# Attention over gathered edges: values weighed from the gathered rows in SBUF, PSUM banks cleared by ScalarE

## The reference, cut to what matters

```python
q = (h @ Wq).reshape(n, H, DK)
k = (h @ Wk).reshape(n, H, DK)
v = (h @ Wv).reshape(n, H, DV)
e = jnp.sum(q[dst] * k[src], axis=-1) / np.sqrt(DK)
m = jax.ops.segment_max(e, dst, num_segments=n)
a = jnp.exp(e - m[dst])
z = jax.ops.segment_sum(a, dst, num_segments=n)
msg = v[src] * (a / (z[dst] + 1e-09))[:, :, None]
agg = jax.ops.segment_sum(msg, dst, num_segments=n)
```

## Time and profile before

| | before |
|---|---|
| median of 3 runs | 6919.58 us (6911.33 to 6929.57) |
| the profiled execution, its own time | 6900.21 us |
| its span | 6898.5 us |
| granted TensorE clock, mean | 0.895 of full |
| TensorE busy (matmul) | 5202.9 us, 75% |
| VectorE busy | 2801.3 us, 41% |
| GpSimd busy | 2226.9 us, 32% |
| ScalarE busy | 1456.7 us, 21% |
| first attention | 2972.3 to 3827 us |
| second attention | 3981 to 4851 us |

### The profile page before, as it was taken

The page is one execution under the profiler, slowest core; times in us unless marked ns, Lnnn a source line. Parts: engine busy times, 40 slices in busy tenths (PEclk is TensorE's granted clock), DMA queues, the critical chain, the costliest instruction groups (busy, mean ns, idle before and its releaser), DMA issues. The chain is left out here.

```text
span 6898.5 us, 86638 instructions
## 1 busy us (share of the span) xinstructions
PE 5202.9 (75%) x22758; PEld 3404.8 (49%) x22807; DVE 2801.3 (41%) x6714; ACT 1456.7 (21%) x3735; POOL 2226.9 (32%) x2209
## 2 busy tenths in 40 slices
PE   3521649898785979568888668888688599999944
PEld 2410337645772459445554445554587544444443
DVE  4271459801323042447666456666323301010142
ACT  1220215401120013113333213333232210000020
POOL 3357120054354515146664055564003200000024
PEclk9999999998797979779998779998788799999957
DMA  0000003253463416468887178887115632424233
GB/s 15 1 1 1 1 26 133 122 176 130 145 200 126 133 53 214 129 201 291 279 285 232 40 240 272 273 275 219 55 44 160 194 126 83 168 80 168 80 87 113
DMA packets 484682, 960.54 MB, mean 139 GB/s; under 512 B 112649, under 2 KB 292468, under 8 KB 481718
## 3 DMA queue, kind: packets, MB, share of 16 engines
q1 hardware_dynamic: 324902, 640.54, 27.7%
q0 software_dynamic: 114208, 281.05, 13.5%
q10 hardware_dynamic: 45296, 35.56, 1.7%
HBM read 737.19 MB, written 219.74 MB: 139 GB/s over the span
## 5 line engine op out<-in xcount | busy, mean ns | idle before, releaser
L1213 PE MATMUL banks<-ring,xn 128*128 128x512 f32 (+1 forms) x3500 | 1348.8, 548 | 121.0 <-PEq L133 104.5
L1040 POOL DMA_INDIRECT rows<-pairs,idxr x832 | 937.1, 1126 | 603.6 <-DVE prod L1991 363.0
L1213 PEld LDWEIGHTS banks<-ring,xn 128*128 128x128 f32 x3500 | 627.9, 191 | 842.7 <-issue 825.7
L2105 PE MATMUL banks<-agg,hotT 128*128 x1664 | 498.6, 435 | 185.2 <-DVE prod L1991 101.2
L394 POOL DMA_INDIRECT dst_table<-nodes_pay,nodes_row x392 | 386.6, 986 | 775.6 <-DVEq L1187 407.2
L394 POOL DMA_INDIRECT bin_table<-bins_pay,bins_row x392 | 403.5, 1029 | 593.1 <-ACTq L802 204.7
L2105 PEld LDWEIGHTS banks<-agg,hotT 128*128 128x128 f32 x1664 | 328.1, 213 | 270.6 <-issue 219.6
L2208 ACT ACTIVATE x<-banks x832 | 325.1, 391 | 477.6 <-PE banks L2121 349.8
L1687 PE MATMUL banks<-second,hT 128*128 x1544 | 390.7, 393 | 41.5 <-DVE bins_pay L1733 15.8
L1672 PE MATMUL banks<-xT,w1r 128*128 128x128 f32 x3088 | 404.2, 284 | 17.1 <-DVE xT L1725 7.9
L1672 PEld LDWEIGHTS banks<-xT,w1r 128*128 128x128 f32 x3088 | 382.9, 200 | 21.1 <-issue 13.5
(11 more groups left out here) (379 smaller groups left out, 7614.7 us busy)
## 6 DMA issues: line engine op xcount, KB each, us to landing
ring<-adjacency SPq DMA_DIRECT2D x145, 1280.0 KB
spill<-rows SPq DMA_DIRECT2D x208, 512.0 KB
vals<-spill SPq DMA_DIRECT2D x208, 512.0 KB
w1r<-in_L_ffn_W SPq DMA_DIRECT2D x114, 512.0 KB
adjacency<-strips SPq DMA_DIRECT2D x13, 3200.0 KB
w1r<-in_L_ffn_w SPq DMA_DIRECT2D x65, 512.0 KB
rows<-home_rows SPq DMA_DIRECT2D x35, 640.0 KB
ring<-adjacency SPq DMA_DIRECT2D x25, 640.0 KB
```

Source lines behind the costliest of these rows:

```text
L1040: nc.gpsimd.indirect_dma_start(rows[:, row, :], None, table, bass.IndirectOffsetOnAxis(ap=idxr[:, at + g:at + g + 1], axis=0))\
L1213: last = nc.tensor.matmul(K.ps[2 * (g % 2) + o][:, 0:wd], x[:, t * D + o * P:t * D + (o + 1) * P], ring.buffer[:, n % R, 0:wd // cols, q * ...
L2105: last = nc.tensor.matmul(queries(c, part)[:, n % 2 * D:(n % 2 + 1) * D], hotT[:, c % 2, n * P:(n + 1) * P], tile_of(q, at[n]), start=True ...
```

## The change

Gathered rows stay in SBUF until their values have been weighed: ten slots of one step each, seven of them in a new buffer and three in `K.xn`, whose content is written to DRAM when the attention starts and read back near its end. `spill` and `vals` are gone. `multiply` writes its products over the keys it read. The indirect DMA reads its indices straight from `edges.idx`, in a plain unrolled loop. The product of noughts is gone: after a bank has been copied to `acc`, ScalarE clears it with a second activation (`iota` times 0). TensorE's four value products, the flip of the weights and `scale`, ScalarE's evacuations, and VectorE's `lower` and register load stand in other places of their step. `before` holds two waves and is wrapped by a small copy every other wave; `peak` and `ends` lie in lent memory.

```diff
+HELD = 7
+LENT = 3
+SLOTS = HELD + LENT
...
+        held = st.sb("held", [P, HELD, GS, 2 * D])
+        lent = K.xn[:, 0:LENT * GS * 2 * D].rearrange("p (j c d) -> p j c d", j=LENT, c=GS)
...
-                gather_rows(nc, pool, edges, K.pairs, rows, idxr, gathered, staged, passed, product, spilled, GS)
+                for i in range(S):
+                    if i == HELD:
+                        pool.wait_ge(parked, 16)
+                    if i >= SLOTS:
+                        pool.wait_ge(weighed, i - SLOTS + 1)
+                    for n in range(GS):
+                        k = GS * i + n
+                        nc.gpsimd.indirect_dma_start(rows(i)[:, n, :], None, K.pairs,
+                                                     bass.IndirectOffsetOnAxis(ap=edges.idx[:, k:k + 1], axis=0))\
+                            .then_inc(gathered[i % SLOTS], 16)
 
             @block.sync
             def _(sp):
+                sp.dma_start(K.parked_norm, K.xn[:, :]).then_inc(parked, 16)
+                sp.wait_ge(weighed, max(i for i in range(S) if i % SLOTS >= HELD) + 1)
+                sp.dma_start(K.xn[:, :], K.parked_norm).then_inc(fetched, 16)
+                sp.wait_ge(fetched, 16)
 
...
                 def multiply(c):
-                    j = c % (RING // GS)
                     dve.wait_ge(queried, c + 1)
-                    dve.wait_ge(gathered[j], 16 * GS * (c // (RING // GS) + 1))
-                    if c >= 2:
-                        dve.wait_ge(scored, c - 1)
+                    dve.wait_ge(gathered[c % SLOTS], 16 * GS * (c // SLOTS + 1))
                     for hh in range(2):
+                        keys = rows(c)[:, 2 * hh:2 * hh + 2, 0:D]
+                        V.tensor_tensor(keys, queries(c, hh)[:, 0:2 * D].rearrange("p (c d) -> p c d", d=D), keys,
+                                        ALU.mult).then_inc(product if hh else halved, 1)
 
...
                 def weigh(g):
                     v, at = g // GW, g % GW * GS * HEADS
                     if g >= MSGS:
                         dve.wait_ge(summed, GS * (g - MSGS + 1))
-                    dve.wait_ge(loaded[g % VALS], 16 * (g // VALS + 1))
                     dve.wait_ge(weighted, v + 1)
+                    V.tensor_tensor(msg[g % MSGS][:, :, 0:DH].rearrange("p (c h) d -> p c h d", c=GS),
+                                    rows(g)[:, :, D:2 * D].rearrange("p c (h d) -> p c h d", d=DH),
+                                    weights[:, v % 2, at:at + GS * HEADS].rearrange("p (c h) -> p c h", c=GS)
+                                    .unsqueeze(3).broadcast_to([P, GS, HEADS, DH]),
                                     ALU.mult).then_inc(weighed, 1)
 
...
+                    if v and at == 0:
+                        link(V.tensor_copy(before[:, 0:1], before[:, 2 * B:2 * B + 1]))
...
+                    if three:
+                        lower(three)
                     if two is not None:
                         shift(two)
...
+                def value(g, n, starts):
+                    k = GS * g + n
+                    if n == 0:
+                        pe.wait_ge(weighed, g + 1)
+                        pe.wait_ge(slotted, g + 1)
+                    if k >= SUMS:
+                        pe.wait_ge(zeroed, k - SUMS + 1)
+                    if k and k % B == 0:
+                        pe.wait_ge(rescaled, k // B)
+                    nc.tensor.matmul(K.banks[:, bass.ds(starts[n], W)], hot[:, g % HOTS, n, :],
+                                     K.spare[g % MSGS][:, n * W:(n + 1) * W],
+                                     start=False, stop=True, skip_group_check=True).then_inc(summed, 1)
 
                 pe.wait_ge(cleared, 1)
                 for i in range(S + LAG):
                         query(i - 1, 0, at)
                     if i < S:
                         to_come = load(mybir.EngineType.PE, edges.chunks.tiles(i), NT - 1)
+                    if g == 0:
+                        pe.wait_ge(cleared, 2)
+                        starts = load(mybir.EngineType.PE, edges.chunks.sums(g), SUM_BANKS)
+                    if g >= 0:
+                        value(g, 0, starts)
                     if two is not None:
                         pe.wait_ge(carried, two + 1)
                         nc.tensor.matmul(spans, G.of_headT[:, :], past[:, :, :].rearrange("p w b -> p (w b)"), start=True,
                     if 0 <= i - 1 < S:
                         query(i - 1, 1, at)
                     at = to_come
+                    if three is not None:
+                        pe.wait_ge(raised, three + 1)
+                        if three:
+                            pe.wait_ge(read, three)
+                        nc.tensor.transpose(flat, over[:, :], K.ident[:, :]).then_inc(returned, 1)
                     if g >= 0:
-                        starts = load(mybir.EngineType.PE, edges.chunks.sums(g), SUM_BANKS)
+                        value(g, 1, starts)
                     if i < S:
                         pe.wait_ge(onehot, i + 1)
                         if i:
                             last = nc.tensor.transpose(turns[:, n * P:(n + 1) * P], hot[:, i % HOTS, n, :], K.ident[:, :])
                         last.then_inc(turned, 1)
                     if g >= 0:
-                        if g == 0:
-                            pe.wait_ge(cleared, 2)
-                        values(g, starts[0:GS], starts[GS:2 * GS])
+                        value(g, 2, starts)
                     if one is not None:
                         pe.wait_ge(ended, one + 1)
                         nc.tensor.matmul(small, G.of_head[:, :], ends[:, :, :].rearrange("p w b -> p (w b)"), start=True,
                                          stop=True).then_inc(moved, 1)
-                    if two is not None:
+                    if g >= 0:
+                        value(g, 3, starts)
+                        if g + 1 < S:
+                            starts = load(mybir.EngineType.PE, edges.chunks.sums(g + 1), SUM_BANKS)
+                    if two:
                         pe.wait_ge(shifted, two + 1)
-                        if two:
-                            pe.wait_ge(framed, two)
-                            nc.tensor.matmul(scale, head_hot[:, :], head_fade[:, :], start=True, stop=True).then_inc(scaled, 1)
-                    if three is not None:
-                        pe.wait_ge(raised, three + 1)
-                        if three:
-                            pe.wait_ge(read, three)
-                        nc.tensor.transpose(flat, over[:, :], K.ident[:, :]).then_inc(returned, 1)
+                        pe.wait_ge(framed, two)
+                        nc.tensor.matmul(scale, head_hot[:, :], head_fade[:, :], start=True, stop=True).then_inc(scaled, 1)
 ...
+                def keep(k, t, start):
+                    act.wait_ge(summed, k + 1)
+                    if k:
+                        act.wait_ge(zeroed, k)
+                    bank = K.banks[:, bass.ds(start, W)]
+                    nc.scalar.activation(tile_of(acc, t, W), bank, ACT.Copy).then_inc(kept, 1)
+                    act.wait_ge(kept, k + 1)
+                    nc.scalar.activation(bank, K.iota[:, 0:W], ACT.Copy, scale=0.0).then_inc(zeroed, 1)
+
                 act.wait_ge(cleared, 2)
                 for i in range(S + LAG):
                     two, three = full(i - 2), full(i - 3)
                     if two:
                         act.wait_ge(carried, two + 1)
                         nc.scalar.activation(fade[:, :], risen[:, :], ACT.Exp, scale=-1.0).then_inc(faded, 1)
-                    if i < S:
-                        act.wait_ge(turned, i + 1)
-                        if i >= 2:
-                            act.wait_ge(queried, i - 1)
-                        nc.scalar.activation(hotT[:, i % 2, :], turns, ACT.Copy).then_inc(copied, 1)
                     if g >= 0:
-                        to = load(mybir.EngineType.Activation, edges.chunks.tiles(g), NT - 1)
-                        ends_in = load(mybir.EngineType.Activation, edges.chunks.kept(g), SUM_BANKS)
-                    if two is not None:
-                        act.wait_ge(shifted, two + 1)
-                        nc.scalar.activation(over[:, :], over[:, :], ACT.Exp).then_inc(raised, 1)
-                    if g >= 0:
-                        for n in range(GS):
-                            k = GS * g + n
-                            act.wait_ge(summed, k + 1)
-                            if k:
-                                act.wait_ge(kept, k)
-                            nc.scalar.activation(tile_of(acc, to[n], W), K.banks[:, bass.ds(ends_in[n], W)],
-                                                 ACT.Copy).then_inc(kept, 1)
+                        keep(GS * g, to[0], ends_in[0])
                     if three is not None:
                         act.wait_ge(returned, three + 1)
                         if three >= 2:
```

(49 more changed lines are left out.)

84 lines of the change are left out of this document (20 added, 64 removed).

## The result

The changed kernel took 6827.34 us (median of 4 runs, 6804.25 to 6837.54) where the kernel before took 6916.42 us on the same chip (4 runs, 6911.33 to 6929.57): ratio 0.986, 95% interval 0.984 to 0.989. The forecast was 6630 us, with a range of 6550 to 6740. So the sign was right and the size a third of what was forecast: 89 us instead of 291. The profiled execution took 6830.38 us, its span 6828.6.

What follows compares the result with a forecast made beforehand. TensorE was taken to set the pace. Each attention: 21 + 31 + 97 x 6.35 + 49 = 717 us, twice that against 1724.7 saving 291, so 6630 us, range 6550 to 6740.

Steps and rivals of the forecast that it cites:

- first six steps: Start of each attention, before any weigh: by four free gathers 5.1 us each, 31 us; up to 25 might come back.
- T = 6.35: Mean steady step in us: two engines at 6.0 to 6.1, plus half of the 0.64 lost per step to waits.
- tail: End of each attention, eight steps of products only at half clock: 59.8 - 8 x 4 x 0.32 = 49 us.
- The step that failed: GpSimd's gathers per step: three free at 1.25 us, one beside a weigh at 2.26, 6.0 in all; ten slots decouple it.
- I am wrong if: Signs of error: step above 6.5 from ScalarE's clearings, GpSimd waiting for L2010, granted clock below 0.8, first weigh after 60 us.
- TensorE: Its steady step without the four products of noughts: 6.9 - 0.84 = 6.06 us, nothing given for shrinking gaps behind products.
- ScalarE: Its copies and 416 new clearings per attention: 1.16 us a `keep`, 4.1 to 5.6 us a step, covered by 0.4 only.
- The detour: Gathered rows' way through DRAM, 41.6% of the DMA engines: already hidden, so nothing booked in the steady steps for removing it.
- The slots: GpSimd's wait for `weigh` of ten steps back: nothing behind it as long as steps take over 2.6 us.
- rival 4: Slower: TensorE's brief stands keep the clock at 1.2 GHz, step 9.5 us, attention 1022, median 7240; chance 0.04.
- Rival 3: Each weigh and one-hot on VectorE blocks gathers for its whole length: step 6.9 us, attention 770, median 6735; chance 0.06.
- Rival 1: The steady steps' stands stay as they are: step 6.7 us, attention 751, median 6697; chance 0.20.

Runs made afterwards that it cites:

- e1: The changed kernel with only the first ten steps gathered, later steps working on what lies in the slots: 6534.24 us on the slower kind of chip.
- e2: The changed kernel with each step's rows loaded by one plain DMA from SyncE instead of four indirect ones from GpSimd: 6463.64 us, slower kind.
- e5: The changed kernel with three gathers per step instead of four after the first ten: 6535.52 us on the slower kind of chip, 6107.82 on the faster.

## Why the prediction was wrong

Its own sum against the changed profile, both attentions, predicted and measured:

| term | predicted | first | second |
|---|---|---|---|
| head, to first `multiply` | 21 | 15.9 | 16.1 |
| first six steps, to first `weigh` | 31 | 62.8 | 62.1 |
| 97 steps | 616 (T = 6.35) | 691.5 (7.13) | 712.2 (7.34) |
| tail | 49 | 44.8 | 45.6 |
| sum | 717 | 815 | 836 |

Together 1651 us against 1434, 217 too much: 172 from T, 63 from the first steps, less 18 from head and tail. The profiled execution is 221 us above the 6609 forecast for it; the rest of the program hardly moved (5177.6 us outside the windows, 5173.8 before). (The tail's own sum, 59.8 - 8 x 4 x 0.32, is 49.6.)

**The step that failed** is GpSimd's: "3 x 1.25 + 2.26 = 6.0 us" was taken as the whole price of its gathers and "ten slots decouple it", so that the terms T = 6.35 and 31 us of first steps held nothing for what they do to TensorE. They measured 7.13 and 7.34, and 62.8 and 62.1. GpSimd's own price was even less than booked, 0.95 to 1.96 us a gather with a mean of 1.08 (405.46 / 376). What was put at nothing is that TensorE's completions come late beside four gathers a step: on the slower kind 6.8 to 7.3 us a step with them and 5.77 with three, two or none, 62 us of first steps with them and 26 to 28 with plain DMAs. The old pace of four gathers in 7.5 us was put down to waits for `multiply` and `spill` alone.

**The sign had been seen and set aside.** The text called the 14.9 us stand of the earlier trace rows implausible in its releaser, and booked the first steps at 31 us with up to 25 to come back. The last item of its list "I am wrong if", over 60 us of head to the first `weigh`, came true with 78.7 us (15.9 + 62.8); so did a step above 6.5, though not by ScalarE's clearings. The stand before a late `weigh` was put down to the weights' place in the order alone; in it ScalarE's copy at 3288.65 starts 1.4 us after the recorded end of its product, where 0.15 is usual in the steps around, so part of it was a late completion as well.

**TensorE** was predicted at 6.06 us, "nothing" given for the gap behind each product. Without late completions the whole step is 5.77 to 5.83 us, and TensorE is busy for only 4.75 of it (460.94 / 97); with noughts on TensorE it is 5.95. So the floor of 6.0 was 0.2 too high and TensorE no longer the limit. That the gap shrank because other work stood between the products fits this, but was not tested alone. On the faster kind the gain is larger than forecast, 347 us; the kernel before has no trace there, so how it divides isn't shown.

**ScalarE** held: 0.39 us a clearing (832 of them), and a `keep` with its clearing every 1.01 us where 1.16 was taken:

```profile
3787.14 0.39 ACT L2159 ACTIVATE x<-banks  x1 [1.04 <-PE banks L2085]
3787.56 0.39 ACT L2161 ACTIVATE banks<-iota 128x264 f32 x1
3788.15 0.39 ACT L2159 ACTIVATE x<-banks  x1 [0.20 <-ACT banks L2161]
```

**The detour** was booked as free. e1 with idle DMA engines and e2 at 0.52 have the same step, so up to that load transfers cost nothing; the 0.85 of the kernel before was not tried. **The slots** did show a wait for L1971, 185 us from 3056 to 3740, which the list named as a sign of error. It is a consequence: e5 on the slower kind has 142 us of it from 3056 to 3560 at 5.77 us a step, and on the faster kind it is absent. **The clock** (0.86 and 0.84 over the attentions) stayed above 0.8, so rival 4 fell; but in the middle stretch it was 0.89 where the kernels without late completions have 0.99 or 1.00, and what that is of the 7.13 is not separated here. **Rival 3**, a gather locked out by a VectorE instruction, comes near the measured step (6.9) for a wrong reason: it needs 1.9 us of blocking a step, and the mean gather, 1.08 us, is only 0.13 longer than one beside nothing; on the faster kind the same instructions share the same SBUF at 5.83. **Rival 1**, the stands stay, was nearest in kind: they stayed and grew, and the time lies 87 us above the range. That the time still fell by 89 us is not to the credit of the sum: its two terms for the steps were too low by 172 and 63 us.

## What to carry to other kernels

When a wait is put down to a releaser that can't be it, find out which engine's completion is late before pricing the change; the stand may be a limit that a faster schedule will hit in every step. Look for the same wait in a part of the trace in which the suspected engine is silent. Waits that are removed also spaced what comes behind them: if an engine issues indirect DMAs, compare their rate before and after, and not only the engine's busy time. Run the unchanged kernel beside every experiment: three of them here looked like cures on a chip on which there was nothing to cure.

## What the runs showed of the hardware that was not expected

- On the slower kind of chip TensorE's completions come late, by up to 20.7 us in the changed kernel and 21.8 us in e1, while GpSimd issues indirect DMAs closely, and by 0.04 us where the last one lay 11 us back. Three per 5.77 us do nothing; four leave 6.8 to 7.3 us a step. Neither half the bytes (6.66) nor half the rows (7.15) cure it, and four plain DMAs from SyncE (5.78) don't cause it.
- Chips differ in it: on two of the six measurements nothing of it shows. It may not be only attention: the first stage has GpSimd's scatters (L387) beside TensorE. The waits there, 0 to 1000 us on the chip of the measurement:

```profile
ACT loT L738 <- remote: 260.8, 10, 55.4
DVE found L766 <- remote: 213.1, 11, 44.1
```

  On the faster kind this stage has no such row, and the first `multiply` comes at 2630.64 us instead of 2991.93: 361 us of what separates the two kinds lie ahead of attention. That these are late completions too is likely by the waits, and wasn't tested.
- Behind the stand of 3.3 us shown above TensorE's granted clock was at its lower level (1.00 before it, 0.50 behind it): four queries took 1.03 us before it and 1.88 behind it.
